# Expert layer of a graph and mixture-of-experts kernel: half-size blocks in pairs, resident weights, and a ring for the up weights

## The reference

```
x = attention(x, adj)               # layer 1: exp(8 tanh(cos/8)) * adj, rows normalised, then a linear map
x = x + experts(layer_norm(x))      # layer 2: 16 experts, 2 per token
x = graph layers(x)                 # layer 3: two steps of top-p attention plus adj
x = x + one expert pair(...)        # layer 4: 8 experts
```

```
y[t] = sum over its two e of  g[t,e] * ( (silu(x[t] @ w1[e]) * (x[t] @ w2[e])) @ w3[e] )
w1, w2: 16 x 128 x 256      w3: 16 x 256 x 128
```

## Time and profile before

| | |
|---|---|
| Time before, median of 3 runs | 850.89 us (850.39 to 857.13) |
| Time of the profiled execution | 847.06 us |
| Its span, first to last instruction | 845.3 us |
| PE busy | 718.9 us (85%) |
| DVE / ACT / POOL busy | 605.8 / 449.7 / 293.7 us |
| Mean granted clock of PE | 0.944 of full speed |
| DMA | 50.36 MB, mean 60 GB/s |

### The profile page before, as it was taken

How to read it: one execution, slowest core, us unless ns; L and a number is a source line. 1 busy time by engine, 2 the same in 40 slices (tenths; PEclk the granted TensorE clock), 3 DMA queues, 4 the chain that set the end, 5 groups by cost and what they waited for, 6 DMA issues and landing times.

```text
span 845.3 us, 15761 instructions
## 1 busy us (share of the span) xinstructions
PE 718.9 (85%) x5287; PEld 546.0 (65%) x5294; DVE 605.8 (72%) x2089; ACT 449.7 (53%) x689; POOL 293.7 (35%) x649
## 2 busy tenths in 40 slices
PE   3799999769999688999999988878678896789893
PEld 2576766439999444677778677765346684787463
DVE  6336656714444468999872699889698998997767
ACT  2366476215555245564663385758696676632153
POOL 4310413465666201112100155163251687870000
PEclk9999999979999899999999999889998997989997
DMA  9999620086887300000000000000000002101001
GB/s 156 188 200 166 123 62 20 30 227 187 233 235 215 125 1 1 1 1 1 2 2 1 1 2 2 2 2 2 0 1 2 1 2 65 38 1 34 1 2 50
DMA packets 82184, 50.36 MB, mean 60 GB/s; under 512 B 42192, under 2 KB 78928, under 8 KB 82096
## 3 DMA queue, kind: packets, MB, share of 16 engines
q1 hardware_dynamic: 64304, 28.35, 14.9%
q0 software_dynamic: 11456, 14.62, 8.8%
q10 hardware_dynamic: 6336, 6.32, 3.0%
HBM read 39.69 MB, written 9.57 MB: 58 GB/s over the span
## 4 chain that ended last, share of the span: by engine, by line
DVE 17%; issue 15%; PE 14%; POOL 8%; POOLq 7%; ACT 3%; DVEq 0%; ACTq 0%
DVE cand L1371 5%; PE bank L2151 3%; DVE big L1608 3%; PE bank L2062 2%; PE bank L2335 2%; PE bank L2134 1%; PE bank L311 1%; PE bank L2348 1%; PE bank L2055 1%; POOLq L1233 1%; DVE cand L1547 1%; DVE big L1478 1%; ACT big L1851 1%; POOLq L1217 1%; POOL bt L1218 1%
## 5 line engine op out<-in xcount | busy, mean ns | idle before, releaser
L2134 PE MATMUL bank<-ident,big 128*128 128x128 f32 x512 | 78.0, 300 | 29.3 <-DVEq L1631 17.9
L2134 PEld LDWEIGHTS bank<-ident,big 128*128 128x128 f32 x512 | 59.6, 150 | 56.3 <-ACT big L1881 22.7
L2055 PE MATMUL bank<-kk,qq 64*128 64x512 f32 x256 | 76.3, 713 | 19.8 <-ACT big L1851 19.2
L1881 ACT ACTIVATE big<-bank 128x512 f32<-128x512 f32 x128 | 70.1, 596 | 42.1 <-PE bank L2134 41.8
L2062 PEld LDWEIGHTS bank<-parts,adjT 128*128 128x128 bf16 x1536 | 86.7, 98 | 2.2 <-issue 2.1
L2062 PE MATMUL bank<-parts,adjT 128*128 128x128 bf16 x1536 | 87.9, 219 | 0.0
L1851 ACT ACTIVATE big<-bank,negm 128x2048 f32<-128x2048 f32 x32 | 62.6, 1956 | 27.1 <-DVE fsc L1658 17.0
L1608 DVE SCALAR_TENSOR_TENSOR big<-big,st 128x2048 f32<-128x2048 f32 x32 | 73.9, 2346 | 2.9 <-PE bank L2134 2.9
L572 DVE TENSOR_TENSOR big<-big,adjT 128x1024 f32<-128x1024 f32 x32 | 39.8, 1248 | 49.3 <-ACT big L731 41.7
L428 POOL DMA_INDIRECT ys_scratch<-big,parts x62 | 60.0, 967 | 37.3 <-ACT big L774 27.3
L858 PEld LDWEIGHTS bank<-xrows,big 128*128 128x128 f32 x512 | 61.8, 195 | 15.2 <-DVE big L572 10.2
(11 more groups left out here) (379 smaller groups left out, 1439.0 us busy)
## 6 DMA issues: line engine op xcount, KB each, us to landing
big<-in_L_ffn_w_dram SPq DMA_DIRECT2D x93, 128.0 KB
big<-in_adj_dram POOLq DMA_DIRECT2D x8, 512.0 KB, 8.6
big<-xs_scratch ACTq DMA_DIRECT2D x31, 132.0 KB
kk<-in_adj_dram POOLq DMA_DIRECT2D x4, 512.0 KB, 13.1
qq<-in_adj_dram POOLq DMA_DIRECT2D x4, 512.0 KB, 13.6
xs_scratch<-hacc SPq DMA_DIRECT2D x9, 132.0 KB, 2.5
xs_scratch<-hacc ACTq DMA_DIRECT2D x8, 132.0 KB, 3.1
res<-in_x_dram SPq DMA_DIRECT2D x4, 256.0 KB, 5.2
```

The lines of the kernel that those rows point to most:

```text
L1881: nc.scalar.activation(MT[:, 4 * q:4 * q + 4, s * P:(s + 1) * P], bank[:, 5 + q % 2, :].rearrange("p (j i) -> p j i", j=4), ACT.Copy).then ...
L2055: nc.tensor.matmul(bank[:, c, :], qq[lo:lo + DA, (g * G + s) * P:(g * G + s + 1) * P], kk[lo:lo + DA, c * CH:(c + 1) * CH], start=True, st ...
L2134: mm = nc.tensor.transpose(bank[:, 5 + q % 2, j * P:(j + 1) * P], mk[:, s, jt * P:(jt + 1) * P], ident[:, :])
```

## The change

Blocks are half as large (`SB` = 128 rows) and PE works on a pair of them at a time, called a unit here (`UR` = 256 rows). There are 48 half blocks and so `NU` = 24 units in place of 31 blocks. Every third half block is the first block of an expert (16 of them), at an address that is known when the program is written; the other `MB` = 32 half blocks (numbered d) go through the tables `block_e` and `block_at`, as all did before. So of three units in a row, the first and the second hold one fixed and one table half each, and the third holds two table halves.

All 16 experts' weights (6.3 MB) are loaded ahead: those of ten experts as soon as layer 1's `adj` has been transposed, the other six when layer 1's last product is formed. For this, `kk`, `qq` and `big` become one array, and small scratch areas move. The up products of a fixed half read the resident weights. Those of a table half read a ring of six buffers, which SP fills with w1 and w2 of its expert, two DMAs of 128 KB (`load_ring`). The down products of a table half read the resident w3 at an address that PE takes from a register (`value_load` on PE, one for each table half).

The rows are read with one DMA for each half (66 KB), two for each unit, and it is SP that issues them (`load_x`), no longer ACT. SP's list for the loop is: six `load_ring`; the waits for the tables, the scatters and the tails; then for each unit `load_x(m)` and behind it those `load_ring` whose turn it is. By the code, 25 ring fills stand between the first six and `load_x(23)`, and one behind it.

```
-        SB = 2 * P
-        MB = (2 * N + E * (SB - 1)) // SB
+        SB = P
+        UR = 2 * SB
+        MB = 2 * E
+        NU = (E + MB) // 2
+        NR = 6
+        def expert_of(m, a):
+            h = 2 * m + a
+            return (h // 3, None) if h % 3 == 0 else (None, h - h // 3 - 1)
+        def unit_of(d):
+            return (3 * d // 2 + 1) // 2
...
+                def load_x(m):
                     k = m % NB
-                    e = bass.ds(sp.value_load(block_e[0:1, m:m + 1], min_val=0, max_val=E - 1), 1)
                     if m >= NB:
-                        sp.wait_ge(d_done, m - NB + 1)
-                    sp.dma_start(wb1[:, k, :], L0_ffn_w1[e].rearrange("a p h -> (a p) h")).then_inc(b_ld[k], 16)
-                    sp.dma_start(wb2[:, k, :], L0_ffn_w2[e].rearrange("a p h -> (a p) h")).then_inc(b_ld[k], 16)
-                    sp.dma_start(wb3[:, k, :, :], L0_ffn_w3[e].rearrange("a (c p) d -> (a p) c d", p=P)
-                                 ).then_inc(b_ld[k], 16)
+                        sp.wait_ge(t_done, m - NB + 1)
+                        sp.wait_ge(w_ready, m - NB + 1)
+                    for a in range(2):
+                        e, d = expert_of(m, a)
+                        if d is None:
+                            rows = slice(e * REG, e * REG + SB)
+                        else:
+                            rows = bass.ds(sp.value_load(block_at[0:1, d:d + 1], min_val=0, max_val=E * REG), SB)
+                        sp.dma_start(xs[:, k, a, :], xs_dram[rows, :]).then_inc(b_xld[k], 16)
+
+                def load_ring(d):
+                    k = d % NR
+                    if d >= NR:
+                        sp.wait_ge(h_done, unit_of(d - NR) + 1)
+                    e = bass.ds(sp.value_load(block_e[0:1, d:d + 1], min_val=0, max_val=E - 1), 1)
+                    sp.dma_start(ring[:, k, 0:H], L0_ffn_w1[e].rearrange("a p h -> (a p) h")).then_inc(r_ld[k], 16)
+                    sp.dma_start(ring[:, k, H:2 * H], L0_ffn_w2[e].rearrange("a p h -> (a p) h")).then_inc(r_ld[k], 16)
...
+                load_experts(slice(0, E_FIRST))
                 sp.wait_ge(tail_set, 1)
                 zero_rows(sp, slice(E * REG, E * REG + SB)).then_inc(zeroed, 16)
+                sp.wait_ge(pm_ready, NQ)
+                load_experts(slice(E_FIRST, E))
                 sp.wait_ge(tail_ready, 1)
                 for e in range(0, E, 2):
                     zero_tail(sp, e)
                 sp.wait_ge(block_ready, 1)
-                for m in range(MB):
-                    load(m)
+                for d in range(NR):
+                    load_ring(d)
+                sp.wait_ge(at_ready, 1)
...
+                ringed = NR
+                for m in range(NU):
+                    load_x(m)
+                    while ringed < MB and unit_of(ringed - NR) + NB <= m:
+                        load_ring(ringed)
+                        ringed += 1
...
-                for m in range(NB):
-                    load_x(m)
                 take_xT(0)
...
+                def down_of(m, a, c):
+                    e, d = expert_of(m, a)
+                    at_ = 2 * H + c * D
+                    return by_expert[:, e, at_:at_ + D] if d is None else weights[:, bass.ds(chosen[d] * EW + at_, D)]
...
+                for m in range(NU):
+                    for a in range(2):
+                        e, d = expert_of(m, a)
+                        if d is not None:
+                            chosen[d] = pe.value_load(block_e[0:1, d:d + 1], min_val=0, max_val=E - 1)
+                    if m + 1 < NU:
                         turn(m + 1)
                     pe.wait_ge(t_out, m + 1)
-                    for w, b in ((wb1, 2), (wb2, 4)):
+                    for at_, b in ((0, 2), (H, 4)):
                         for c in range(HC):
-                            mm = nc.tensor.matmul(bank[:, b + m % 2, c * SB:(c + 1) * SB], w[:, m % NB, c * P:(c + 1) * P],
-                                                  xsT[:, m % 2, :], start=True, stop=True)
+                            for a in range(2):
+                                mm = nc.tensor.matmul(bank[:, b + m % 2, c * UR + a * P:c * UR + (a + 1) * P],
+                                                      up_of(m, a, at_ + c * P), xsT[:, m % 2, a * P:(a + 1) * P],
+                                                      start=True, stop=True)
                     mm.then_inc(h_done, 1)
```

More of the change, by code:

```diff
@@ L262, in zero_rows @@
         def zero_rows(eng, at_):
-            return eng.dma_start(xs_dram[at_, :].rearrange("(p a) d -> p (a d)", p=P), tail)
+            return eng.dma_start(xs_dram[at_, :], tail)
         def zero_tail(eng, e):
@@ L273, in build @@
              "rsum_in"))
-        b_ld, b_xld, b_st = ([sem(f"{v}{k}") for k in range(NB)] for v in ("b_ld", "b_xld", "b_st"))
+        b_xld, b_st = ([sem(f"{v}{k}") for k in range(NB)] for v in ("b_xld", "b_st"))
+        w_ld = sem("b_w_ld")
+        r_ld = [sem(f"b_r_ld{k}") for k in range(NR)]
         b_got = [sem(f"b_got{c}") for c in range(NC)]
@@ L332, in _, with load_experts @@
                                                slot[u % NS][:, s, :]).then_inc(adj_turned[u % TS], 16)
-                def load(m):
+                def load_experts(es):
+                    for k, w in enumerate((L0_ffn_w1, L0_ffn_w2)):
+                        sp.dma_start(by_expert[:, es, k * H:(k + 1) * H], w[es].rearrange("e p h -> p e h")
+                                     ).then_inc(w_ld, 16)
+                    for c in range(HC):
+                        sp.dma_start(by_expert[:, es, 2 * H + c * D:2 * H + (c + 1) * D],
+                                     L0_ffn_w3[es, c * P:(c + 1) * P].rearrange("e p d -> p e d")).then_inc(w_ld, 16)
@@ L345, in _ @@
+                for k in range(TS):
+                    sp.wait_ge(adj_turned[k], 16 * TPC * (NC * NC // TS))
+                load_experts(slice(0, E_FIRST))
                 sp.wait_ge(tail_set, 1)
-                sp.wait_ge(adj_ld[NS - 1], 16 * (NC * NC // NS))
                 zero_rows(sp, slice(E * REG, E * REG + SB)).then_inc(zeroed, 16)
+                sp.wait_ge(pm_ready, NQ)
+                load_experts(slice(E_FIRST, E))
                 sp.wait_ge(tail_ready, 1)
@@ L351, in _ @@
                 sp.wait_ge(block_ready, 1)
-                for m in range(MB):
-                    load(m)
+                for d in range(NR):
+                    load_ring(d)
+                sp.wait_ge(at_ready, 1)
+                for k in range(2):
+                    sp.wait_ge(scattered[k], NT * 16)
+                sp.wait_ge(zeroed, 16 * (E + 1))
+                ringed = NR
[4 more added lines that the diff above has]
+                        ringed += 1
+                assert ringed == MB
                 def row(v):
@@ L640, in target @@
                     k, v = m % NB, xs[:, m % NB, :, :]
[L641 to L644, removed]
+                    halves = slice(2 * m, 2 * m + 2)
+                    dve.wait_ge(b_xld[k], 32 * (m // NB + 1))
+                    ch.mark(nc.vector.tensor_tensor(k1[:, m % 2, :], v[:, :, E0], rows_h[:, BE_, halves], ALU.not_equal))
+                    ch.link(nc.vector.scalar_tensor_tensor(out=t1[:, m % 2, :], in0=v[:, :, E0], scalar=0.0,
+                                                           in1=rows_h[:, TRASH_, halves], op0=ALU.is_lt, op1=ALU.mult))
                     ch.mark(nc.vector.scalar_tensor_tensor(out=dest0[:, m % 2, :], in0=k1[:, m % 2, :], scalar=float(N),
@@ L756, in take_xT @@
                         act.wait_ge(h_done, m - 1)
[L757 to L765, removed]
+                    nc.scalar.activation(xsT[:, m % 2, :], bank[:, m % 2, 0:UR], ACT.Copy).then_inc(t_out, 1)
                 def take_y(m):
@@ L775, in take_y @@
                                              scale=wy[:, m % NB, a:a + 1]).then_inc(y_out, 1)
-                act.wait_ge(at_ready, 1)
-                for k in range(2):
-                    act.wait_ge(scattered[k], NT * 16)
-                act.wait_ge(zeroed, 16 * (E + 1))
-                for m in range(NB):
-                    load_x(m)
                 take_xT(0)
-                for m in range(MB):
-                    if m + 1 < MB:
+                for m in range(NU):
+                    if m + 1 < NU:
                         take_xT(m + 1)
-                    if m and m + NB - 1 < MB:
-                        load_x(m + NB - 1)
                     act.wait_ge(h_done, m + 1)
@@ L957, in turn, with up_of @@
                     mm.then_inc(t_done, 1)
+                def up_of(m, a, at_):
+                    e, d = expert_of(m, a)
+                    return by_expert[:, e, at_:at_ + P] if d is None else ring[:, d % NR, at_:at_ + P]
+                def down_of(m, a, c):
+                    e, d = expert_of(m, a)
+                    at_ = 2 * H + c * D
```

(4 more changed lines are left out.)

103 lines of the change are left out of this document (60 added, 43 removed).

## The result

| | before | changed |
|---|---|---|
| Median of 20 runs each | 851.36 us | 860.38 us |
| Ratio, 95% interval | | 1.0076 (1.0048 to 1.0105) |
| Profiled execution (span) | 847.06 us (845.3) | 855.16 us (853.1) |

The change makes the kernel 0.76% slower, 6.5 us of 851 (the interval is 4.1 to 8.9 us). The ratio is of fast runs alone, 17 of the changed kernel's 20, as three took over 1.5% more than its fastest; the medians in the table are of all 20 and differ by 9.0 us. The profiled executions differ by 8.1 us. Forecast was +6.3 us.

What follows compares the result with a forecast made beforehand. PE bounds the loop before (2.84 us a block), SP's list after (4.07 us a unit against PE's 2.91). Load_y comes at 289.4 instead of 283.10, so 850.89 + 6.3 = 857.2 us; range 843 to 872.

Steps and rivals of the forecast that it cites:

- The forecast case: Block loop: SP's list becomes the bound and PE waits for rows in most units; 849 to 866 us, chance 0.70.
- PE's need for a unit: Block loop on PE: a unit takes 2.91 us, so 24 units need 70 us instead of 88, alone 18 less.
- load_y: Read behind the block loop: starts at 289.4 instead of 283.10, +6.3 us.
- SP's average of 4.07 us a unit: Block loop on SP: ring fills and half blocks' DMAs take 4.07 us a unit, against 2.91 that PE needs.
- The first transpose: Start of the block loop on PE: at 191.9 instead of 185.52, so the loop starts 6.4 us late.
- The last rows' issue: End of SP's list in the block loop: the last unit's rows are issued at 275.0.
- What else moves, at nothing: Outside the loop's sum: weight loads, larger tables, ACT's lost issues and SP's constant loads cost nothing; work behind load_y unchanged.
- PE's register loads at nothing: Block loop on PE: 32 register loads, bound 0 to 0.93 us a unit, taken as 0 since PE will have slack.
- The resident weights at nothing: Ahead of the block loop: loading 6.3 MB needs 28 us in two parts, both covered, so no cost.
- Rival 1: Block loop: SP keeps up and PE stays the bound; -12.8 us, 838 us, chance 0.15.
- Rival 2: Block loop: PE loses its clock while it waits; 13.6 us more than forecast, 871 us, chance 0.10.
- Rival 3: Block loop: register loads or register addresses stall PE by over 1.2 us a unit; 7 us more, 864, chance 0.05.

Runs made afterwards that it cites:

- the second experiment: Against the changed kernel, SP fills two ring buffers instead of six before issuing the first rows, same work; ratio 1.0072 to the kernel before.

## Why the prediction was right

The forecast case came: SP's list bounds the loop. By its steps:

- **PE's need for a unit**, put at 2.91 us, is 2.90 where PE leads. Halving the up products costs no more than the 0.07 us of the sum, and the seven fewer blocks are the gain that the rows-on-ACT kernel realises: its loop, tails to load_y, is 96.5 us against 114.4 before (283.10 - 168.73), 17.9 less where the text said 18.
- **SP's average of 4.07 us a unit** is 4.06 over the three units shown and 4.07 over fifteen. This step carries the forecast; adding 16 register loads (+10.1 us), dropping 32 DMAs (-8.8), shuffling the list (+0.6) and moving the rows off it (-22.9, all by the loop) answer to it.
- **The first transpose**, put at 191.9, is at 191.01, and the second experiment shows that the 6.4 us of late start, which the text gave some room, is not a cost of its own: it is part of the same list.
- **The last rows' issue**, put at 275.0, is at 274.6; **load_y**, put at 289.4, is at 289.22. That these agree to 0.4 us and less is in part luck, as several errors cancel. The tails began 1.15 us late, where the text allowed 0.1. A ring fill takes (186.93 - 179.03) / 5 = 1.58 us, not 1.65, which over 31 fills gives 2.2 us back. SP's waits for PE are 1.0 us, not 1.7. Landing took 1.8 us at the end, not 2.5. Against them stand two issues of 0.96 (210.77) and 1.247 us, 1.5 us together above the usual 0.34 to 0.38; the kernel before has three such (0.83 to 1.21), and the sum left them out. And behind the last up products, which started at 279.33 and not 280.4, came 9.9 us and not 9.0: that term was taken without a backlog of POOL, and POOL had one (its last stores are 0.30 us apart, at 285.65 and 286.92).
- **What else moves, at nothing** held less well. The loop itself is 5.0 us longer (119.3 against 114.4), not 6.2; ahead of it stand the 1.15 us, and behind it 1.7 us (563.9 against 562.2), so that the profiled execution took 8.1 us more and not 6.3. The ratio of the runs, +6.5 us with an interval from 4.1 to 8.9, can't tell 5 from 6.3; that it meets the forecast to 0.2 us is luck.
- **PE's register loads at nothing** held, but by less than the text suggests: "since PE will have slack" was not the reason, as the rows-on-ACT kernel has none and still runs at 2.90. That they are hidden behind queued products fits this, and twice as many are not hidden.
- **The resident weights at nothing**: their DMAs land in 6.0 to 11.5 us (the page's medians for the four sizes), they are issued between 118 and 157 us, the DMA engines are at 0.02 from 165 to 170 us, and PE shows no wait for them.
- **Rival 1** (SP keeps up) fell. **Rival 2** (the clock) came once: 

```profile
255.59 1.96 PE L1054 MATMUL bank<-arena 128*128 128x128 f32 x16
...
260.51 0.69 PE L1005 MATMUL bank<-ident,arena 128*128 128x128 f32 x2 [2.06 <-DMA arena<-xs_scratch]
260.99 3.34 PE L1054 MATMUL bank<-arena 128*128 128x128 f32 x16
265.06 0.38 PE L1005 MATMUL bank<-ident,arena 128*128 128x128 f32 x2
```

Behind a wait of 2.06 us one unit's up products took 3.34 us instead of 1.96, and the clock of that stretch is 0.83; as SP was the bound, the loss was made up by the next units, which did not wait. Its price of 13.6 us was too high, since the clock came back within one unit: in the kernel with the list in another order the clock is 0.83 in three stretches of 10 us, and load_y comes 0.1 us later than in the changed kernel. The length of a wait alone doesn't tell: with the doubled register loads PE waited 3.60 us ahead of 273.78, and the clock of 270 to 280 us stayed at 1.00. **Rival 3** was not seen.

Of the 1.15 us by which the tails began late, 0.7 go with the clock. PE sums columns of `adj` ahead of the last ranks, 16 products that took 3.61 us before and 5.82 in the changed kernel (PE's timelines and stretches, the kernel before first):

```profile
159.35 3.61 PE L939 MATMUL bank<-adjT,onesb 128*1 128x512 bf16 x16
...
160.00:165.00 5.00, 2.97 (x14) 1.01 (x12) 4.42 (x33) 1.85 (x5) 2.35 (x3) 1.00 0.12 41
```

```profile
160.43 5.82 PE L988 MATMUL bank<-adjT,onesb 128*1 128x512 bf16 x16
...
160.00:165.00 5.00, 5.00 (x14) 1.75 (x14) 4.43 (x32) 1.85 (x5) 2.60 (x3) 0.51 0.89 260
```

DVE's next step waits 0.88 us for PE behind them, 0.17 before. Another 0.25 us had been lost by 157 us, and the rest are DVE's larger tables. In seven of the eight kernels with resident weights the granted clock is 0.51 to 0.76 from 160 to 165 us, where the kernel before has 1.00; in the eighth (one register load more in each fixed half) it is 1.00 as well, and its tails start at 170.19, later still. So the change may have a part in that clock, but neither is this shown, nor that the late start hangs on it alone.

The Trainium skill's sentence on issuing engines (DMA: Bandwidth & Descriptors, Issuing engines are not separate DMA queues) speaks of one DMA, and for one it holds here: an issue takes 0.34 to 0.38 us, the landing 2.0 to 2.1 (the page's medians). What it leaves out is the sum of a serial list: with the register loads in it, moving the rows to ACT was worth 22.9 us of the loop, and the reading by which it "would cost next to nothing" is wrong here.

## What to carry to other kernels

Count each issuing queue like an engine: its DMAs (0.44 to 0.48 us each here, start to start) and its register loads (0.63 to 0.8 us), times their number in a period, against the period of the engine that bounds the loop. A change that gives PE less work by cutting blocks smaller can give the queue more, and the queue shows in no busy column. Before moving DMAs onto a queue, add up its list; here another order of the same list didn't help, another queue with room did.

## What the runs showed of the hardware that was not expected

A DMA whose source and destination are both in SBUF took 0.52 us to issue, one from DRAM of half the size 0.34 to 0.38. Whether the place or the size does it was not separated.

Of PE's register loads, the change's one or two in a unit of 2.90 us left no trace; doubled, four cost 0.75 to 0.93 us and two from 0.1 to 0.8; the record of one is 0.30 us long plus 0.15 of arithmetic.

The part behind load_y is the same program in all kernels, yet it took from 562.2 us (before) to 572.3 (ring fills from the resident weights) in single profiled executions, with 563.9 in the changed kernel. A single span therefore can't separate these kernels by less than about 1%; the position of load_y can, and the ratios of several runs do. What varies is for the most part one place: between 300 and 352 us behind `load_y` in the kernel before, the same work (DVE's instructions from the 700th to the 600th before the end) takes 52 to 54 us in six of the nine profiles and 61 to 62 in three (one register load more, fewer rows ahead of ACT's first copy, ring fills from the resident weights), and these are the three whose part behind `load_y` is over 570 us. The granted clock from 320 to 360 us behind `load_y` is 0.77 to 0.83 in those three and 0.87 to 0.93 in the six others. Why it differs there is open.
